# A two-way state-space scan: one of two TensorE convolutions moves to VectorE, and the gram products change their order

## The reference

```
def _L3_attn_b_ref(u, W_in, conv_w, conv_b, dt_bias, A_log, Dp, fc_D_w, norm_w, W_out):
    zxbcdt = einsum('bld,ed->ble', u, W_in)          # z: 256, xBC: 512, dt: 8 features
    xc = depthwise_conv(xBC, conv_w, 7 taps) + conv_b
    xBC = silu(xc)                                    # x: 256; B and C of both directions: 4 x 64
    # per direction: state = state * exp(A*dt) + x_t B_t ; y_t = state . C_t
    y = y_fw + y_bw + x * (x @ fc_D_w.T + Dp)
    y = norm_w * (y / sqrt(mean(y*y) + EPS)) * silu(z)
    return einsum('ble,de->bld', y, W_out)
```

## Time and profile before

| | us |
|---|---|
| median of 3 runs (lowest, highest) | 7737.04 (7718.37, 7741.0) |
| the profiled execution, its own time | 7739.17 |
| its span in the trace | 7737.40 |
| the stage in the trace (first tap weights to its last VectorE instruction) | 6197.4 to 6637.0 |
| TensorE busy over the whole span | 76% |
| VectorE busy over the whole span | 54% |
| ScalarE busy over the whole span | 38% |

### The profile page before, as it was taken

One profiled execution on the slowest core, in us unless ns is written; L12 is line 12 of the kernel. 1 busy time (PEld: TensorE's weight loads), 2 busy tenths in 40 slices (PEclk: granted clock), 3 DMA queues, 4 the chain that ended last, 5 costly groups with the idle time before them and its releaser, 6 DMA issues. The chain is left out here.

```text
span 7737.4 us, 121045 instructions
## 1 busy us (share of the span) xinstructions
PE 5852.5 (76%) x45636; PEld 2850.6 (37%) x45838; DVE 4148.7 (54%) x6437; ACT 2938.2 (38%) x6433; POOL 1964.7 (25%) x1790
## 2 busy tenths in 40 slices
PE   5556667786578876666568999978878889688787
PEld 3445351115352222222223545534434334244343
DVE  4333636662437745778854444445455466555554
ACT  1002223463235541443310222246546455365464
POOL 0004142113142201444422001024234011242341
PEclk6557887897788888787787787889989989899898
DMA  1001022212121100000003122111011000110110
GB/s 46 4 28 56 30 62 75 66 42 69 50 66 39 39 17 14 0 0 0 0 7 62 38 49 54 29 43 45 20 53 45 9 6 0 39 45 23 53 45 20
DMA packets 261164, 269.01 MB, mean 35 GB/s; under 512 B 113600, under 2 KB 190656, under 8 KB 258688
## 3 DMA queue, kind: packets, MB, share of 16 engines
q1 hardware_dynamic: 250368, 240.26, 12.0%
q0 software_dynamic: 10240, 21.25, 0.8%
HBM read 122.59 MB, written 71.66 MB: 25 GB/s over the span
## 5 line engine op out<-in xcount | busy, mean ns | idle before, releaser
L2250 PE MATMUL ps<-s_l2b_hc,ident 128*128 128x512 f32 x512 | 362.4, 848 | 331.0 <-DVE s_l2b_hc L2413 331.0
L2198 POOL TENSOR_TENSOR s_l2b_Bx<-s_l2b_du,s_l2b_B 128x512 f32<-128x512 f32 x256 | 406.5, 1609 | 473.9 <-ACT s_l2b_B L2320 410.8
L1827 PE MATMUL ps<-s_l3l_hs,s_l3l_wqk 128*128 128x512 f32 x512 | 330.9, 754 | 223.5 <-DVE s_l3l_prod L1978 156.5
L1954 ACT ACTIVATE s_l3l_probs<-ps,s_l3l_biases,s_l3l_q_inverse 128x128 f32<-128x128 f32 x1024 | 454.1, 458 | 58.1 <-DVE s_l3l_biases L2024 57.8
L2405 DVE TENSOR_TENSOR_SCAN s_l2b_state<-s_l2b_decay,s_l2b_Bx 128x512 f32<-128x512 f32 x256 | 389.8, 1562 | 155.2 <-ACT s_l2b_decay L2326 113.9
L2022 DVE TENSOR_REDUCE s_l3l_negmax<-ps 128x4 f32<-128x512 f32 x256 | 176.5, 690 | 524.3 <-PE ps L1866 524.3
L1057 DVE TENSOR_REDUCE s_L3a_negmax<-ps 128x1 f32<-128x128 f32 (+3 forms) x512 | 236.3, 488 | 362.9 <-PE ps L893 360.6
L1802 POOL TENSOR_TENSOR s_l3l_probs<-s_l3l_probs,s_l3l_inverse 128x512 f32<-128x512 f32 x256 | 266.6, 1042 | 635.4 <-DVE s_l3l_inverse L2004 633.0
L1035 ACT ACTIVATE s_L3a_pt<-ps 128x256 f32<-128x256 f32 (+3 forms) x512 | 195.2, 434 | 529.3 <-PE ps L893 527.5
L638 DVE TENSOR_REDUCE s_L1a_negmax<-ps 128x1 f32<-128x512 f32 x512 | 316.4, 682 | 139.7 <-PE ps L501 139.3
L908 PE MATMUL ps<-ks,s_L3a_qs 40*128 40x256 f32 (+3 forms) x1024 | 359.8, 610 | 31.3 <-DVE s_L3a_kvsq L1072 16.5
(11 more groups left out here) (663 smaller groups left out, 13292.4 us busy)
## 6 DMA issues: line engine op xcount, KB each, us to landing
s_l3l_qk<-s_l3l_rope SPq DMA_DIRECT2D x1024, 64.0 KB
scratch_rope<-s_L3a_rope SPq DMA_DIRECT2D x32, 512.0 KB, 2.8
ks<-scratch_parts SPq DMA_DIRECT2D x384, 32.0 KB
s_L3a_qs<-scratch_rope SPq DMA_DIRECT2D x64, 128.0 KB
ks<-scratch_rope SPq DMA_DIRECT2D x64, 128.0 KB
s_L0e_slots<-scratch_sent SPq DMA_DIRECT2D x16, 396.0 KB, 5.6
s_L1e_slots<-scratch_sent SPq DMA_DIRECT2D x16, 396.0 KB, 6.0
scratch_square<-s_L1a_rows SPq DMA_DIRECT2D x24, 256.0 KB, 3.0
```

What stands on the lines that cost most here:

```text
L1827: mm = pe.matmul(out, t["wqk"][:, 2 * e + ab, :], tokens, start=True, stop=True)
L1954: act.activation(t["probs"][:, U % (LAG + 1), k, :], ps[:, U % 2, P * k:P * (k + 1)], ACT.Exp, bias=t["biases"][:, U % (LAG + 1), k:k + 1] ...
L2198: pool.tensor_tensor(t["Bx"][:, n % 2, k, :], t["du"][:, b % 2, k, :], t["B"][:, n % 2, :], ALU.mult).then_inc(s["bx_ready"], 1)
L2250: pe.matmul(ps[:, 4 + k, :], g["ident"][:, :], t["hc"][:, n % 2, k, :], start=(n == 0), stop=(n == STATES - 1)).then_inc(s["summed"], 1)
```

## The change

Group 2 (the B rows) is convolved on VectorE instead of TensorE. VectorE's three convolutions of batch b+1 now stand in units 0, 1 and 2, for groups 2, 0 and 1 in this order; the one of unit 2 comes behind `scale` and ahead of products 3. ScalarE applies silu to groups 3, 2 and 0 in unit 2, and to group 1 in unit 3, between the exponentials and the gram copies. Gram items now alternate between forward and backward: forward 512, backward 512, forward 384 + 128, backward 384 + 128, forward 256, backward 256. `taps` halves to 7 matrices, `conv` grows to three groups, and the counts of the semaphores `conv_done` and `xbc_ready` go from two to three per batch (`TURN` gives the place of each group). The core of the diff:

```diff
-    GRAMS = [(0, (0,)), (0, (1, 3)), (0, (2,)), (1, (3,)), (1, (2, 0)), (1, (1,))]
+    GRAMS = [(0, (0,)), (1, (3,)), (0, (1, 3)), (1, (2, 0)), (0, (2,)), (1, (1,))]
+    TURN = {2: 0, 0: 1, 1: 2}
...
-            items += [("conv", b + 1, k) for k in (2, 3)] if following else []
+            items += [("conv", b + 1, 3)] if following else []
...
                     d, sts = GRAMS[item[2]]
-                    for k in (2, 3):
-                        taken(pe, ("conv", b, k))
+                    taken(pe, ("conv", b, 3))
+                    pe.wait_ge(s["xbc_ready"], START + 3 * b + TURN[2] + 1)
...
-                    pe.wait_ge(s["xbc_ready"], START + 2 * b + k + 1)
+                    pe.wait_ge(s["xbc_ready"], START + 3 * b + TURN[k] + 1)
...
-            convolved(0)
+            take(("conv", 0, 3))
+            convolved(0, (2, 0, 1))
...
-                        for k in (2, 3):
-                            take(("conv", b + 1, k))
-                        convolved(b + 1)
+                        take(("conv", b + 1, 3))
+                        convolved(b + 1, (2, 0))
                         for item in side_work(b, 2):
                             take(item)
                 if q == 3:
+                    if b + 1 < BATCH:
+                        convolved(b + 1, (1,))
                     for item in side_work(b, 3):
                         take(item)
...
-            convolution(0, 0)
-            convolution(0, 1)
+            for k in (2, 0, 1):
+                convolution(0, k)
...
                 if q == 0 and following:
-                    convolution(b + 1, 0)
+                    convolution(b + 1, 2)
                 if q == 1:
                     if b:
                         keep_mean(b - 1)
                     if following:
-                        convolution(b + 1, 1)
+                        convolution(b + 1, 0)
                 if q == 2 and b:
                     scale(b - 1)
+                if q == 2 and following:
+                    convolution(b + 1, 1)
```

More of the change, by code:

```diff
@@ L2912, in two_way_scan @@
     SLOT = [{0: 0, 1: 4 * P, 3: 7 * P, 2: 8 * P}, {3: 0, 2: 4 * P, 0: 7 * P, 1: 8 * P}]
-    GRAMS = [(0, (0,)), (0, (1, 3)), (0, (2,)), (1, (3,)), (1, (2, 0)), (1, (1,))]
+    GRAMS = [(0, (0,)), (1, (3,)), (0, (1, 3)), (1, (2, 0)), (0, (2,)), (1, (1,))]
+    TURN = {2: 0, 0: 1, 1: 2}
     ROWS3 = 96
     tensors = {"in_w": ([P, 6, P], F32), "dt_w": ([P, 4, P], F32), "conv_w": ([P, 4, 7], F32), "conv_b": ([P, 4], F32), "dt_b": ([P, 1], F32), "A": ([P, 1], F32), "back": ([P, 1], F32),
-               "D": ([P, 2], F32), "fc": ([P, 2, 2, P], F32), "norm_w": ([P, 2], F32), "out_w": ([P, 2, P], F32), "pick": ([P, 32], F32), "pickb": ([P, 32, P], BF16), "taps": ([P, 2, 7, P], F32),
-               "mean": ([P, P], F32), "padded": ([P, 4, T + 6], F32), "silu_z": ([P, 2, 2, T], F32), "conv": ([P, 2, T], F32), "xbc": ([P, 2, 4, T], F32),
+               "D": ([P, 2], F32), "fc": ([P, 2, 2, P], F32), "norm_w": ([P, 2], F32), "out_w": ([P, 2, P], F32), "pick": ([P, 32], F32), "pickb": ([P, 32, P], BF16), "taps": ([P, 7, P], F32),
+               "mean": ([P, P], F32), "padded": ([P, 4, T + 6], F32), "silu_z": ([P, 2, 2, T], F32), "conv": ([P, 3, T], F32), "xbc": ([P, 2, 4, T], F32),
                "u": ([P, 2, T], F32), "e": ([P, 2, T], F32), "log": ([P, 2, T], F32), "rows": ([P, 2, T], F32), "one": ([P, T], F32), "parts": ([P, 2, T], BF16),
@@ L2954, in grams @@
         return [("gram", b, n) for n in range(len(GRAMS))] + [("turn", b, k) for k in range(2)]
-    FIRST = entering(0) + [("conv", 0, 2), ("conv", 0, 3), ("z", 0, 0), ("z", 0, 1)] + grams(0) + [("cols", 0)]
+    FIRST = entering(0) + [("conv", 0, 3), ("z", 0, 0), ("z", 0, 1)] + grams(0) + [("cols", 0)]
     LAST = leaving(BATCH - 1, "fc") + leaving(BATCH - 1, "mean") + leaving(BATCH - 1, "out")
@@ L3055, in side @@
                     if b == 0:
-                        pe.wait_ge(s["taps_made"], START + 14)
+                        pe.wait_ge(s["taps_made"], START + 7)
                         pe.wait_ge(s["pool_ready"], START + 2)
                     for tap in range(7):
-                        mm = pe.matmul(out, t["taps"][:, k - 2, tap, :], t["padded"][:, k, tap:tap + T], start=(tap == 0), stop=(tap == 6))
+                        mm = pe.matmul(out, t["taps"][:, tap, :], t["padded"][:, k, tap:tap + T], start=(tap == 0), stop=(tap == 6))
                 elif what == "gram":
                     d, sts = GRAMS[item[2]]
-                    for k in (2, 3):
-                        taken(pe, ("conv", b, k))
+                    taken(pe, ("conv", b, 3))
+                    pe.wait_ge(s["xbc_ready"], START + 3 * b + TURN[2] + 1)
                     rows, at = slice(64 * d, 64 * d + 64), 0
@@ L3161, in take @@
                     k = item[2]
-                    if b and k >= 2:
+                    if b and k == 3:
                         ready(act, ("conv", b - 1, k))
                     elif b:
-                        act.wait_ge(s["conv_done"], START + 2 * (b - 1) + k + 1)
+                        act.wait_ge(s["conv_done"], START + 3 * (b - 1) + TURN[k] + 1)
                     taken_by(act.activation(t["padded"][:, k, 3:3 + T], out, ACT.Copy), item)
@@ L3182, in take, with convolved @@
                     taken_by(act.activation(t["G"][:, b % 2, d, at:at + size], out[:, 0:size], ACT.Copy), item)
-            def convolved(b):
-                for k in range(2):
-                    act.wait_ge(s["conv_done"], START + 2 * b + k + 1)
+            def convolved(b, ks):
+                for k in ks:
+                    act.wait_ge(s["conv_done"], START + 3 * b + TURN[k] + 1)
                     if b > 1:
+                        ready(act, ("gram", b - 2, len(GRAMS) - 1))
+                        ready(act, ("gram", b - 2, len(GRAMS) - 2))
                         ready(act, ("fc", b - 2, 1))
@@ L3220, in _ @@
                 take(item)
-            for k in (2, 3):
-                take(("conv", 0, k))
-            convolved(0)
+            take(("conv", 0, 3))
+            convolved(0, (2, 0, 1))
             for item in [("z", 0, 0), ("z", 0, 1)] + grams(0):
@@ L3254, in _ @@
             vec.wait_ge(s["loaded"], START + LOADED)
-            for k in range(2):
-                for tap in range(7):
-                    vec.tensor_scalar(t["taps"][:, k, tap, :], g["ident"][:, :], t["conv_w"][:, 2 + k, tap:tap + 1], None, ALU.mult).then_inc(s["taps_made"], 1)
+            for tap in range(7):
+                vec.tensor_scalar(t["taps"][:, tap, :], g["ident"][:, :], t["conv_w"][:, 3, tap:tap + 1], None, ALU.mult).then_inc(s["taps_made"], 1)
             vec.wait_ge(s["A_ready"], START + 1)
@@ L3265, in convolution @@
                 if b:
-                    vec.wait_ge(s["xbc_ready"], START + 2 * (b - 1) + k + 1)
+                    vec.wait_ge(s["xbc_ready"], START + 3 * (b - 1) + TURN[k] + 1)
                 conv = t["conv"][:, k, :]
@@ L3274, in convolution @@
                         ins = vec.scalar_tensor_tensor(out=conv, in0=shifted, scalar=weight, in1=conv, op0=ALU.mult, op1=ALU.add)
-                        own(ins, *((s["conv_done"], 2 * b + k + 1) if tap == 6 else ()))
-            convolution(0, 0)
-            convolution(0, 1)
+                        own(ins, *((s["conv_done"], 3 * b + TURN[k] + 1) if tap == 6 else ()))
+            for k in (2, 0, 1):
+                convolution(0, k)
             vec.wait_ge(s["log_ready"], START + 1)
```

## The result

The changed kernel takes 7757.96 us (median of 20 runs, 7743.12 to 7775.97), the kernel before in 20 runs 7730.17. The ratio of the means is 1.0034, interval 1.0024 to 1.0043: by it the kernel is slower by 26 us, at least 19 and at most 33. In the traces the stage (first GpSimd instruction to the last `add_out`) grew from 447.32 to 467.86 us, by 20.5, which lies inside that interval. The difference of the two spans (7737.4 and 7741.6) is smaller: the other stages, which the change doesn't touch, came out 16 us shorter in the second of these two executions.

A forecast was written before the change was run, and what follows sets the result against it. The prediction took VectorE's work up to `add_out`, then TensorE's tail, as the bound. Six batches by 3.0 us, plus 2.35 at stage start, less 3 in batch 0, gave +17.35 us: 7755, range 7732 to 7778.

The forecast's parts named there:

- The ring: One batch, combine to combine: VectorE's work up to `add_out`, then TensorE's tail; `add_out` ends 3.0 us later.
- 38.40 instead of 35.40: VectorE's stretch from combine to the end of `add_out`, in us, after the change and before it.
- Stage start: VectorE starts group 2 2.9 us earlier but has 5.24 more to do before the softplus chain: 2.35 us later.
- Batch 0: First batch, without combine: the third convolution fills VectorE's wait for exponentials of unit 3; 3 us earlier, ends 1 and 6.
- The tail: End of `add_out` to next combine, 13.27 us: no change taken; ends 3.9 us less, 1.6 more.
- both pulls: On the tail: paired grams, up to 3.9 us less; lower TensorE clock after longer idling, 1.6 more.
- TensorE idle for 5 to 6 us ahead of gram 1: Sign of being right: TensorE waits about 5.8 us ahead of the second gram, ended by `add_out`.
- Sum: Whole kernel: six batches by 3.0, plus 2.35, less 3, gives +17.35 us; 7755 forecast, chance 0.55.
- TensorE as the bound: Rival: TensorE's work sets the pace, so seven batches each lose 6.15 us; 7699, chance 0.08.
- The gram pairs: Rival: opposite-direction grams overlap and shorten the tail by 3.9 us in six batches; 7733, or 7745 at half; chance 0.15.
- The clock's rival: Rival: TensorE's lower clock reaches into `values` and `fc`, 5.3 us a batch; 7789, or 7772 at half; chance 0.22.

The follow-up runs named there:

- e_gate: Changed kernel with `add_out` on VectorE moved ahead of products 3 instead of behind them; 7734.35 us, 1.0009 of the kernel before.
- e_late: Changed kernel with the third VectorE convolution moved behind `add_out` and its silu behind the gram copies; 7714.74 us, 0.9985 of the kernel before.
- e_twice: Changed kernel with TensorE's remaining convolution computed twice over in batches 1 to 7; 7757.72 us, 1.0037 of the kernel before.
- e_oldgrams: Changed kernel with the gram items in their old order, all forward, then all backward; 7760.09 us, 1.0039 of the kernel before.
- e_grams_only: Kernel before with the alternating gram order alone, both convolutions staying on TensorE; 7727.40 us, 1.0000 of the kernel before.
- e_warm: Changed kernel with the first gram of batches 2 to 7 computed five times over into the same bank; 7736.84 us, 1.0011 of the kernel before.

## Why the prediction was right, point by point

- *The ring.* Right. "38.40 instead of 35.40" came out as 38.31, in all six batches within 0.02; no idle time ahead of products 3; `add_out` ends TensorE's wait. e_gate and e_late show that it is the place of the convolution and not its work that costs, and e_twice that the seven matmuls lie beside VectorE's stretch.
- *Stage start.* 2.35 forecast, 2.54 measured.
- *Batch 0.* 3 us earlier forecast, 4.45 measured (41.49 to 37.04). The convolution's move alone gives 2.5 of it (e_oldgrams takes 39.03 here), and the gram order the other 2.0; e_grams_only, with the order alone, gains 1.5 (39.96). With seven matmuls put back, e_twice loses 6.16 here.
- *The tail, "no change".* This was the term that was mis-sized: 0.83 us more in each of six rings, 5.0 in all. I had seen both pulls and let them cancel. e_oldgrams, which has the longer wait but the old order, sets them apart. The wait with its lower clock costs 1.15 us in a ring (tail 13.70 to 14.85, all of it between the second gram and the first turn: 6.17 to 7.32 as a mean of six), where I had put 1.6 as the end. The new order gives back 0.32 (14.85 to 14.53), where I had put 3.9 as the end. Its price of 0.46 came from `values`, whose column halves I had taken as the nearest row. The overlap itself is there, but the two banks take most of it back, as I had feared in that same paragraph ("gram 3 waits for the copy of gram 1"). Against the full clock the low one is worth far more: e_warm has tails of 10.2 at 1.00 and of up to 14.2 where it falls. It had cost the kernel before most of that already, so the change added little.
- *TensorE idle for 5 to 6 us ahead of gram 1.* Right in two of the six tails (5.55), too long in the other four (3.90 to 4.94). In the tail shown the clock had fallen behind the wait for products 2 (3.11 us), so that the output projection took 3.58 us instead of 1.98 and ended later.
- *Sum.* 17.4 forecast, 20.5 in the traces, 26 by the ratio with an interval that reaches down to 19. The forecast of 7755 lies 3 us from the measured 7758, but a part of that is luck: the median of the kernel before turned out 7 us lower in 20 runs than in the first three. The measured 7758 lies within 7714 to 7760, to which I gave 0.59; by the ratio the change is a little over the 0.3% from which these bounds come, with 0.3% inside its interval.
- *Rivals.* TensorE as the bound fell with e_twice, but for batch 0. The gram pairs overlap, but did not shorten the tail by the forecast 3.9 us, or by half of it. The Trainium skill, TensorEngine Tiling, section on the theoretical speedup, gives up to two times for a small dimension of 64 or less. Here the eight grams, with their copies, went from 9.03 us to 7.21, 1.25 times. The clock's rival was half right: the lower level did reach into `values` (3.53 us in this tail, 2.37 at the full clock), but the first `fc` product had the full clock again.

What was not tried: more PSUM banks for the grams, so that a pair need not wait for the copies of the pair ahead of it.

## What to carry to other kernels

An engine's idle time is only worth something where it lies: before work is put on an engine with room, cut its round at the instruction that others wait for, and see whether the room is ahead of it or behind it. The busiest engine of a stage need not be in its ring; here TensorE, at 93% of a window, could lose or get back 6 us in each full batch without an effect on the ring. Where a small instruction frees a shared buffer, its place in the queue is worth more than its length.

## What the runs showed of the hardware that I had not expected

In e_warm the tail took 10.2 us where TensorE's granted clock stayed at 1.00 and 12.7 to 14.2 us where it fell to 0.50, and useless matmuls that filled the wait ahead of it took 2.6 us off the mean ring (50.21 instead of 52.84). Float32 matmuls on the two halves of the partitions ran side by side, the second 0.48 us behind the first and without slowing it; with two PSUM banks, each of which has to be copied before its next use, the eight grams still took 7.21 instead of 9.03 us, and not half.
